# A four-layer transformer kernel: the issue order of its last two layers written out piece by piece for every engine

## What is computed

```python
x = x + _L2_attn_ref(_layernorm(x), W_qkv, W_o)       # window of 64: |i - j| <= 32, 16 heads of 8
x = x + _L2_ffn_ref(_layernorm(x), w_gate, w_up, w_down)   # silu(gate) * up, int weights dequantised
x = x + _L3_attn_ref(_layernorm(x), wq, w_down, wk_up, wv_up, wo)  # rope, latent k/v, causal by pages of 32
x = x + _L3_ffn_ref(_layernorm(x), gate_w, w1, b1, w2, b2)  # one expert of eight for each token
```

## Time and profile before

| | us |
|---|---|
| median of three runs | 1451.46 |
| lowest, highest | 1445.09, 1454.06 |
| the profiled execution | 1445.91 |
| its span, first to last instruction | 1444.1 |
| stage of L2 and L3 | 550.5 to 1316 |

### The profile page before, as it was taken

How to read it: one execution, slowest core, us unless ns; L and a number is a source line. 1 busy time by engine, 2 the same in 40 slices (tenths; PEclk the granted TensorE clock), 3 DMA queues, 4 the chain that set the end, 5 groups by cost and what they waited for, 6 DMA issues and landing times.

```text
span 1444.1 us, 39308 instructions
## 1 busy us (share of the span) xinstructions
PE 1108.9 (77%) x16860; PEld 816.5 (57%) x16860; DVE 823.0 (57%) x2347; ACT 569.5 (39%) x991; POOL 459.4 (32%) x540
## 2 busy tenths in 40 slices
PE   5899937889874594677788887988888887762896
PEld 3677726777763373444455554655556564442785
DVE  6477764567775013346648576584857665733232
ACT  2133102445452131314264462736456462450342
POOL 3033331344464003222222313333141303112486
PEclk9899968999996797787899899999999999876998
DMA  9940014534140421112111120222122110102695
GB/s 375 411 161 18 18 59 150 182 102 128 36 146 24 109 59 53 46 42 59 44 47 47 49 63 19 56 57 62 47 57 56 33 36 11 52 18 80 149 231 113
DMA packets 86175, 126.57 MB, mean 88 GB/s; under 512 B 14577, under 2 KB 67186, under 8 KB 85586
## 3 DMA queue, kind: packets, MB, share of 16 engines
q1 hardware_dynamic: 69842, 107.93, 23.8%
q0 software_dynamic: 11936, 14.04, 4.3%
q10 hardware_dynamic: 4224, 2.10, 0.5%
HBM read 53.10 MB, written 44.97 MB: 68 GB/s over the span
## 4 chain that ended last, share of the span: by engine, by line
PE 27%; DVE 19%; ACT 8%; issue 4%; POOL 3%; DMA 2%; SPq 2%; another core or an unknown queue 1%; POOLq 0%; DVEq 0%; ACTq 0%
DVE mx L1558 9%; ACT MW L1821 5%; PE ps L1022 2%; PE ps L806 2%; PE ps L1008 2%; PE ps L923 2%; PE ps L820 2%; PE ps L914 2%; PE ps L980 1%; DVE mx L1549 1%; PE ps L836 1%; PE ps L915 1%; DVE bst L1056 1%; DVE X L1084 1%; PE ps L837 1%
## 5 line engine op out<-in xcount | busy, mean ns | idle before, releaser
L1558 DVE TENSOR_REDUCE mx<-ps 128x2 f32<-128x1024 f32 (+3 forms) x176 | 188.7, 1122 | 33.8 <-PE ps L953 33.7
L1821 ACT ACTIVATE MW<-ps 128x1024 f32<-128x1024 f32 x160 | 154.5, 1029 | 78.0 <-PE ps L965 77.8
L1958 POOL DMA_INDIRECT xs<-xr,sidu x96 | 95.8, 998 | 138.5 <-DVE sidu L1217 100.3
L1901 POOL TENSOR_SCALAR rst<-bmv 128x4 f32<-128x4 f32 x64 | 15.9, 248 | 305.1 <-DVE bmv L1059 304.3
L980 PE MATMUL ps<-MW,Vp 128*16 128x128 f32 x2560 | 87.1, 277 | 3.7 <-ACT MW L1821 3.5
L1982 POOL DMA_INDIRECT out_dram<-qf,toku x46 | 71.5, 1554 | 37.8 <-DVE toku L1613 29.3
L953 PE MATMUL ps<-K,Q 64*128 64x512 bf16 (+3 forms) x512 | 62.9, 320 | 22.4 <-DVE mx L1558 15.4
L1549 DVE TENSOR_REDUCE mx<-ps 128x8 f32<-128x768 f32 x64 | 58.0, 950 | 31.5 <-PE ps L862 22.9
L557 PE MATMUL ps<-W,xr 128*128 128x128 f32 x192 | 38.1, 333 | 48.9 <-DVE xr L1069 35.9
L1813 ACT ACTIVATE MW<-ps 128x1024 f32<-128x1024 f32 x64 | 63.5, 1027 | 26.9 <-PE ps L885 24.9
L980 PEld LDWEIGHTS ps<-MW,Vp 128*16 128x16 f32 x2560 | 63.7, 97 | 15.2 <-ACT MW L1821 4.8
(11 more groups left out here) (347 smaller groups left out, 2695.7 us busy)
## 6 DMA issues: line engine op xcount, KB each, us to landing
xs<-hb SPq DMA_DIRECT2D x48, 528.0 KB, 14.3
MW<-l_moe_dram SPq DMA_DIRECT2D x19, 768.0 KB
MW<-l_moe_dram SPq DMA_DIRECT2D x23, 578.0 KB
Q<-spl SPq DMA_DIRECT2D x48, 128.0 KB
K<-spl SPq DMA_DIRECT2D x48, 128.0 KB
Q<-spm SPq DMA_DIRECT2D x48, 128.0 KB
K<-spm SPq DMA_DIRECT2D x48, 128.0 KB
MW<-l_moe_dram SPq DMA_DIRECT2D x16, 256.0 KB
```

Of the source, the lines that this page charges most:

```text
L1558: V.tensor_reduce(out=mx[1][:, :, s0:s0 + ns, t], in_=p.rearrange("p (e n) -> p e n", e=2)[:, :, 0:ns * nk].rearrange("p e (s k) -> p e s ...
L1821: A.activation(P3[k % 2][:, 1024 * half:1024 * half + 1024], p, ACT.Exp).then_inc(drained[u], 1)
L1958: G.indirect_dma_start(out=xs[L], out_offset=bass.IndirectOffsetOnAxis(ap=sidu[:, 4 * b + t:4 * b + t + 1], axis=0), in_=src[:, t, 0:128 i ...
```

## The change

`STEPS2` and its `lanes` call are replaced by `sequences` with a written list for each engine. Every engine still runs the same pieces, as often as before (672 on PE, 472 on DVE, 320 on ACT, 112 on POOL, 32 on SP), and no piece's code changes. SP's list is the same as before. Of the others, 349 places on PE, 181 on DVE, 115 on ACT and 48 on POOL hold another piece than before, mostly by one to five places. The interleaving now differs from batch to batch.

```diff
-STEPS2 = [
-    ("l2_get", dict(POOL=42.32)),
-    ("l2_add", dict(DVE=57)),
...
-ORDER2 = lanes(STEPS2, 74.5)
+ORDER2 = sequences({
+    "PE": """
+        l2a_n l2_q l2a_n l2_v l2_m0 l2_m1 l2_m2 l2_m3 l2_q l2_n2 l2_e0 l2_e1 l2_o0 l2_o1 l2_e2 l2_e3 l2_o2 l2_t0 l2_t1 l2_o3 l2_t2 l2_t3 l2_u
...
+    "POOL": """
+        l2_get l2a_s l2_get l2_p1 l2_p2 l2a_s l2_n1 l2_get l2_p1 l2_p2 l2a_s l2f_s l3a_s l2_get l3_q l3_k l3_p1 l3_p2 l2_n1 l2a_s l2_p1 l2_p2
+        l2f_s l2_get l3_n1 l3a_s l3_q l3_k l3_p1 l3_p2 l2a_s l2_n1 l2_p1 l2_p2 l2_get l2f_s l3_n1 l3f_s l3a_s l3_q l3_k l3_p1 l3_p2 l2_n1
...
```

181 lines of the change are left out of this document (81 added, 100 removed).

## The result

The changed kernel takes 1474.26 us (median of 4 runs, 1466.64 to 1478.25) against 1448.28 us (4 runs, 1444.81 to 1454.06) for the kernel before beside it: ratio 1.0165, 95% interval 1.0129 to 1.02. It is slower by 1.65%; 1435.1 was predicted, with 1451 as the upper end. The profiled execution has a span of 1476.3 us against 1444.1.

A forecast was written before the change was run, and what follows sets the result against it. L3's maxima phases were taken as set by DVE, those between by PE, slowed beside gathers. Terms -15.0 - 5.0 + 2.6 + 1.0 + 0 = -16.4 us, stepped down from the 1451.46 us median, gave 1435.1 us; range 1422 to 1451.

The forecast's parts named there:

- The gathers: POOL's gathers of batches 4, 5, 6 leave `l2_m2`, whose matmuls they stop: -2.0, -7.0, -6.0, together -15.0 us.
- The -2.0 for batch 4: `l2_get.4` leaves `l2_m2.2`, but DVE's `l2f_o.1` ahead of `l2_m0.2` delays drains and uses up most of the win.
- the rival's "against it": Rival that stops travel with the gathers into `l2_o3` (0.22, about 1445 us); against it, `l2_o3` is mostly through by then.
- PE's pieces behind the first maxima: `l3_e8`, `l3_e9`, `l2_q` move behind L3's first maxima, so DVE's phase starts earlier: -5.0 us, bounds 0 and -8.0.
- Start-up: Swapping `l2f_o.0` and `l2_m0.1` delays `l3_m0.0`, and the copy of `l2_n2.1` waits: +2.6 us, bounds 0 and +4.
- Scatters: `l3t_x.1` and `l3t_x.3` move from `l2_m0` to the maxima's start, beside dense `l2_e`: +1.0 us, bounds -1.6 and +3.
- The rest: Other exchanges, one to five places, mostly move work by less than the idle time beside it: 0, bounds -5 and +5.
- the maxima starve: Rival: in batches 3 to 6, `l2_e` or `l3_b8` ahead of single maxima leaves DVE dry, +24 us, 1459 us; chance 0.09.
- The rule from the Trainium skill: Engines fetch straight programs themselves, mostly hidden; by it stops are no price of other traffic and the gathers' -15.0 is zero.
- the cheap phase: Phase 1045 to 1090 between maxima, without a gather: 45.0 us against 51 to 53, with four or more POOL instructions fewer.

The follow-up runs named there:

- gathers3: Kernel before with only POOL's gathers of batches 4, 5 and 6 moved to their places in the changed list: 1432.76 us against 1450.17, ratio 0.9885.
- pool_router: Changed kernel with batch 6's gather behind `l2f_s.3`, `l2_p2.5` ahead of `l2f_s.4`, and DVE's `l2_m3` drain ahead of `l3t_m`: 1458.04 us, 1.0076 of the kernel before.
- heads_moved: gathers3 with PE's pieces put behind the first maxima as in the changed kernel: 1430.12 us, 0.9889 of the kernel before.
- the last pair: Kernel before and changed kernel, neither edited, side by side on chip D, without stops: 1405.65 and 1444.32 us, ratio 1.0273.
- scatter_back: Changed kernel with scatters `l3t_x.1`, `l3t_x.3` and `l3t_x.4` put back behind `l3_n1`: 1462.9 us, 1.0094 of the kernel before.
- three_put_in: gathers3 with batch 6's gather behind `l2_p1.4`, `l3t_x.1` behind `l2a_s.6`, and DVE's `l3t_m.3` ahead of `l2_m3.6`: 1434.31 us, 0.9923 of the kernel before.
- four_undone: Changed kernel with the edits of pool_router and scatter_back and PE's pieces put back ahead of the first maxima: 1461.45 us, 1.0097 of the kernel before.
- pool_back: four_undone with POOL's whole list as in gathers3, on chip C: 1446.64 us, 1.0282 of the kernel before.
- maxima_only: gathers3 with four_undone's order in the maxima phases of batches 1 to 6 alone, on chip C: 1419.43 us, 1.0103 of the kernel before.
- head_b2: Changed lists up to the start of `l3_m0.2`, then the order of the kernel before: 1445.67 us against 1450.17, ratio 0.9975.

## Why the prediction was wrong

- **The gathers, -15.0: the term was right (-17.4 alone), one of the three places was not.** `l2_m2.2`, `.3` and `.4` take 1.35, 1.05 and 1.55 us in the changed kernel, and r0 and r1 shrink by 4.2 and 10.6. (How the -15.0 is shared among the batches was not right: gathers3 gives 9.4, 8.9 and 6.0 in r0 to r2 and takes some back elsewhere. The -2.0 for batch 4 counted on DVE's new order, which gathers3 leaves out.) But the gather of batch 6 met `l2_o3.3` and cost 10.0 us in m2 (pool_router). What failed here is the rival's "against it", that by the new place `l2_o3` is mostly through. It was argued from the order of before; the diff puts `l2_o3.3` behind `l2_t2.3` on PE and `l2_p2.4` ahead of `l2_o3.3` on ACT, so the two move towards each other. `l2_m2.5` didn't stay at 6 us either (1.22): the gather of batch 7 began at 983.67, as it ended, and fell into `l3_e1.3`.
- **PE's pieces behind the first maxima, -5.0: nothing.** The idle time ahead of the first maximum is gone, as forecast, and comes back behind the second one (2.99 us ahead of `l3_m2.2`, up to 6.91 in heads_moved). Both runs, putting it back and putting it in, measure no difference beyond their intervals. The bound of 0 held; the value taken did not.
- **Start-up, +2.6:** `l3_m0.0` came 0.5 us later in the first pair; counted from the start of `l2_get.1` it is 0.1 earlier there and 1.2 later in the last pair. Too large, and harmless.
- **Scatters, +1.0: about 6 to 11 us** in the changed kernel (scatter_back, on one chip with stops), and about nothing in three_put_in (+2.4 and -2.9). The rows chosen showed only PE's stops; that DVE and ACT can be late too was in the trace of the kernel before, in ACT's four waits of 1.8 us beside the gathers, and was overlooked.
- **The rest, 0 with bounds of 5: +29 us where there are stops (four_undone against gathers3, one chip), +42 on a chip without (pool_back).** This is the step that failed and decides. Split by ratios, the measured +1.65% is -1.15% for the gathers (0.9885), +2.1% for the rest (1.0097 against 0.9885) and +0.7% for the places that four_undone puts back (1.0165 against 1.0097), of which the gather in `l2_o3.3` and the scatters are the main part. Order alone costs in both kinds of stretch: 14.7 us in the maxima, 26.3 in the others, each taken by itself; in the changed kernel of chip D, where the pieces moved behind the first maxima shift time from the one kind to the other, 19.1 and 14.1. I reasoned that most pieces move by less than the idle time beside them. But in both kinds of stretch one engine is close to its limit and the three PSUM units tie the others to it, so that an exchange that takes a piece past its drain can cost both engines, and a wait can bring the clock down as well; the waits in m2 show this, for single exchanges in r1 to r6 it is argued. Nearly 300 pieces change places in the lists of PE, DVE, ACT and POOL, and all but a dozen had been summed up as none.
- **The rival "the maxima starve"** (0.09, 1459 us) had the direction and a part of the mechanism: DVE idles behind `l2_e` pieces, 2.4 us at a time, and maxima_only is 14.7 us slower where 24 was the price. Its places were not right. Of batches 3 to 6, where nothing disturbs (D), only m3 loses over 4.1 us (7.6; m4 to m6 0.4, 0.4 and 1.8), m2 with 6.2 was not named, and the first waits in m2 and m3 stand behind the pieces that the prediction had counted as a gain. The loss in the stretches between was in no rival. No rival reached 1474.
- **The rule from the Trainium skill** ("Runtime: NRT & Kernel Launch", "Instruction fetch mechanics") would have set the gathers' term to zero. On the two chips with stops it fails (0.9885 and 0.9866 with the gathers moved, nothing else); on chip D its result holds (1.0013), and on C the traces have no stops. No run shows whether the stops have to do with fetching at all.
- **A reading of the earlier trace rows:** the prediction gives the cheap phase four or more POOL instructions fewer than the dear ones. It has two fewer than the phase from 787 (22 against 24) and six fewer than the other two; nothing in the sum rests on it.

What stays open: why two chips stop PE beside an indirect DMA and two don't; POOL's four instructions take the same 4.9 us on all. Which single exchanges in r1 to r6 carry the 26 us. And how much of head_b2's lead is real.

## What to carry to other kernels

Don't cost a rewritten order of some hundreds of pieces by its three or four visible moves: where one engine leads and few buffers tie the engines together, the many exchanges of one or two places were worth 29 to 42 us here, and the three gathers, the largest of the visible moves, 17. Undo by stretches, not by ideas: comparing the length of each stretch told more than the total, since most stretches repeated to 0.3 us where totals spread by 10; where one with the same lists does not, look at its clock first. And a gain from avoiding stops beside gathers has to be measured on more than one chip.

## What the hardware showed that was not expected

- Indirect DMAs of POOL (gather or scatter, four instructions, 4.9 us) stop PE's dense rows of small matmuls on some chips: `l2_m2.4` 6.0 us against 1.1, `l2_o3.3` 5.2 against 1.09, `l2_o1.3` 3.4, each with stops of mostly 0.4 to 0.5 us every few matmuls. On chips C and D the same pieces run at full speed, and the kernel before takes 1405 us instead of 1445 to 1450.
- On the same chips DVE and ACT are late, too: 1.6 and 1.8 us behind PE's result beside a scatter, ACT 1.8 us beside each gather of the kernel before, marked "remote"; in the stage of the three profiles on chip C and the three on chip D there is no such wait.
- A stretch in which PE was busy 0.77 of 3 us was followed by about 7 us at half clock with PE fully busy.
